# A mixture of experts whose token lists are made inside the expert stage: one list three experts ahead, places in eight rows of 64

## The reference

```
x = x + attention_relative(layernorm(x))
x = x + mixture(layernorm(x))
x = x + attention_window(layernorm(x))
x = x + mixture(layernorm(x))
```

```
scores = softmax(flat_x @ gate_w.T).T              # 16 x 4096
topk_weight, topk_idx = top_k(scores, C)           # each expert takes its 512 best tokens
xg = flat_x[topk_idx]                              # 16 x 512 x 256
h  = gelu(xg @ Wg.T) * (xg @ Wu.T)                 # hidden width 1024
eo = (h @ Wd.T) * topk_weight[..., None]
out = zeros.at[topk_idx].add(eo) + (gelu(x @ Sg.T) * (x @ Su.T)) @ Sd.T
```

## Time and profile before

| | before |
|---|---|
| median of three runs | 4274.7 us (4270.0 to 4282.5) |
| profiled execution: own time | 4275.8 us |
| profiled execution: span | 4274.0 us |
| mean granted TensorE clock | 0.942 |
| TensorE busy | 3662.2 us (86%), 32904 matmul records |
| VectorE busy | 2491.0 us (58%) |
| ScalarE busy | 1835.0 us (43%) |
| GpSimd busy | 780.0 us (18%) |
| DMA | 424 MB, mean 99 GB/s |

### The profile page before, as it was taken

The page is one execution under the profiler, slowest core; times in us unless marked ns, Lnnn a source line. Parts: engine busy times, 40 slices in busy tenths (PEclk is TensorE's granted clock), DMA queues, the critical chain, the costliest instruction groups (busy, mean ns, idle before and its releaser), DMA issues. The chain is left out here.

```text
span 4274.0 us, 91482 instructions
## 1 busy us (share of the span) xinstructions
PE 3662.2 (86%) x32904; PEld 2899.8 (68%) x32904; DVE 2491.0 (58%) x5053; ACT 1835.0 (43%) x3752; POOL 780.0 (18%) x714
## 2 busy tenths in 40 slices
PE   4899999999967848999956999888999695699998
PEld 3566666666556747888844777777777585588887
DVE  4466666666645695555544555444554467655554
ACT  1466666666612204444423444444444230244443
POOL 0122222222200003333310000000010000133332
PEclk9999999999988968999978999999999697799999
DMA  4566655665543204444331000000000420244442
GB/s 176 143 169 166 173 165 166 171 174 168 153 151 125 76 0 158 125 122 120 95 89 77 16 13 11 12 14 13 12 11 13 160 76 23 104 119 118 121 125 44
DMA packets 383916, 423.99 MB, mean 99 GB/s; under 512 B 172896, under 2 KB 323296, under 8 KB 370016
## 3 DMA queue, kind: packets, MB, share of 16 engines
q1 hardware_dynamic: 223840, 319.05, 22.8%
q10 hardware_dynamic: 135168, 67.13, 5.7%
q0 software_dynamic: 24576, 33.57, 4.9%
HBM read 269.37 MB, written 150.27 MB: 98 GB/s over the span
## 5 line engine op out<-in xcount | busy, mean ns | idle before, releaser
L2146 ACT ACTIVATE a_prob<-a_ps_s,a_low 128x512 f32<-128x512 f32 x512 | 319.0, 689 | 43.6 <-DVE a_low L2361 43.3
L2007 PE MATMUL a_ps_p<-a_ident,a_prob 128*128 128x128 f32 x2048 | 310.5, 285 | 24.9 <-ACT a_probT L2122 12.2
L2361 DVE TENSOR_REDUCE a_low<-a_ps_s 128x2 f32<-128x1024 f32 x256 | 313.5, 1225 | 8.8
L2221 POOL TENSOR_TENSOR a_below<-a_probT,a_upper 128x512 f32<-128x512 f32 x128 | 164.3, 1284 | 739.9 <-ACT a_probT L2122 370.4
L2007 PEld LDWEIGHTS a_ps_p<-a_ident,a_prob 128*128 128x128 f32 x2048 | 217.5, 141 | 119.0 <-issue 82.9
L2122 ACT COPY a_probT<-a_ps_p 128x512 f32<-128x512 f32 x352 | 194.1, 589 | 161.6 <-PE a_ps_p L2007 144.9
L1476 ACT ACTIVATE b_prob<-b_score,b_low 128x256 f32<-128x256 f32 (+1 forms) x512 | 240.6, 473 | 34.7 <-PE b_ps_p L1418 23.6
L1428 PEld LDWEIGHTS b_ps_o<-b_v,b_probT 128*128 128x128 f32 x1792 | 227.2, 191 | 9.9 <-issue 0.9
L1428 PE MATMUL b_ps_o<-b_v,b_probT 128*128 128x64 f32 x1792 | 228.3, 267 | 0.7 <-DVE b_o L1562 0.7
L1549 DVE CUSTOM_DVE_ANT_0 b_score<-b_ps_s,b_bias 128x256 f32<-128x256 f32 (+1 forms) x512 | 185.2, 389 | 56.5 <-PE b_ps_s L1409 37.2
L2360 DVE TENSOR_TENSOR a_ps_s<-a_ps_s,a_win 128x320 f32<-128x320 f32 (+1 forms) x256 | 135.0, 527 | 139.2 <-PE a_ps_s L2040 133.4
(11 more groups left out here) (400 smaller groups left out, 10581.3 us busy)
## 6 DMA issues: line engine op xcount, KB each, us to landing
a_win<-band SPq DMA_DIRECT2D x128, 384.0 KB, 4.9
prob<-a_prob ACTq DMA_DIRECT2D x128, 384.0 KB, 3.6
xnT<-n_xnT SPq DMA_DIRECT2D x32, 512.0 KB, 3.2
shift<-a_gbias SPq DMA_DIRECT2D x64, 256.0 KB, 2.0
a_shifted<-shift SPq DMA_DIRECT2D x256, 64.0 KB, 2.6
a_bins<-prob ACTq DMA_DIRECT2D x128, 128.0 KB, 4.5
fe_gT<-in_WgT SPq DMA_DIRECT2D x16, 1024.0 KB, 4.9
fe_uT<-in_WuT SPq DMA_DIRECT2D x16, 1024.0 KB, 5.3
```

The source lines that it names most:

```text
L2007: last = nc.tensor.transpose(bank[:, c * P:(c + 1) * P], prob[:, t % 2, h, 32 + c * P:32 + (c + 1) * P], ident[:, :])
L2146: nc.scalar.activation(prob[:, t % 2, h, 32:32 + T], ps_s[pair][:, r, :], ACT.Exp, bias=low[:, h:h + 1]).then_inc(exped, 1)
L2221: nc.gpsimd.tensor_tensor(below[:, t % 2, :, :], probT[:, t % 2, :, t * P:(t + 1) * P], upper[:, :].unsqueeze(1).to_broadcast([P, HG, P]), ...
L2361: nc.vector.reduce_max(low[:, 2 * pair:2 * pair + 2], both[:, :, :], AX.X, negate=True).then_inc(maxed, 1)
```

## The change

`route_stage` is deleted. Its set-up part (counts, scans, places, turning back) stands at the head of the expert stage's VectorE and TensorE programs; its per-expert part is a set of small steps spread over the eight steps of an expert, for the list of expert e + 3 (AHEAD = 3). Lists 0, 1 and 2 are made before VectorE's first product, between the splits of expert 0's weights and tokens. A place is now cut into place mod 64 (LOW) and place / 64 (8 hits), so that a list takes 32 matmuls of 24 weight columns by 64 moving columns; two more small float32 matmuls against the identity then place the 24 x 64 result on 128 partitions. `onehot` is written in quarters of 8 blocks. One PSUM bank `ps_x` serves both halves of the turned tokens (k = 0 at j = 4, k = 1 at j = 5), and the freed bank holds `ps_r` with the counts, `ps_f` and `ps_s`. GpSimd's gather of an expert waits for its list. The scratch tiles of the set-up lie in tiles that the experts use later. Both tables of the counts are loaded ahead of the identity, and the weights behind the five tables.

```diff
-def route_stage(nc, tag, const, scores, st, thr, slot_token, slot_weight):
...
+    LOW = 64
+    HITS = CAP // LOW
+    COLS = 3 * HITS
+    AHEAD = 3
+    QUARTERS = 4
+    M = NT * B // QUARTERS
...
-        X_STEP = 5
+        X_STEP = 4
+        FOUND_STEP = 3
+        TAKE_STEP = 7
...
+            for tile, dram in loads[0:2]:
+                sp.dma_start(tile, const[dram]).then_inc(const_in, 16)
...
+            for tile, dram in loads[2:]:
+                sp.dma_start(tile, const[dram]).then_inc(const_in, 16)
             for m in range(3):
                 load(0, m)
...
             def gather(e, q):
+                hold(pool, list_ready, e + 1, held)
                 take_index(0, e, q)
...
+            def transpose_rows(i, q, e, k):
+                if k == 0:
+                    pe.wait_ge(gathered[q], DONE * i + DONE)
+                pe.wait_ge(x_split, KC * e + KC + k)
+                for t in range(CT):
+                    last = nc.tensor.transpose(ps_x[:, t * P:(t + 1) * P], xg[:, q, t, k * P:(k + 1) * P], ident[:, :])
+                last.then_inc(x_T, 1)
+            def find(r, quarter):
+                if quarter == 0:
+                    pe.wait_ge(value_ready, 3 * r + 3)
+                    if not (isinstance(r, int) and r == 0):
+                        pe.wait_ge(list_ready, r)
+                pe.wait_ge(hot_ready, QUARTERS * r + quarter + 1)
+                for m in range(M * quarter, M * quarter + M):
+                    last = nc.tensor.matmul(ps_f, value[:, m, :, :, :].rearrange("p a v c -> p (a v c)"), onehot[:, m, :],
+                                            start=(m == 0), stop=(m == NT * B - 1))
+                if quarter == QUARTERS - 1:
+                    last.then_inc(found_ready, 1)
+            def place_slots(r):
+                pe.wait_ge(found_taken, r + 1)
+                for a in range(2):
+                    last = nc.tensor.matmul(ps_s[LOW * a:LOW * a + LOW, :, :].rearrange("p v c -> p (v c)"), found[:, :],
+                                            ident[0:COLS, 3 * CT * a:3 * CT * a + 3 * CT], start=True, stop=True)
+                last.then_inc(listed, 1)
...
+                    if first and j == 1:
+                        for quarter in range(QUARTERS):
+                            find(AHEAD - 1, quarter)
+                        place_slots(AHEAD - 1)
+                    if j == 0 and is_within(i, q, 1, E - AHEAD):
+                        place_slots(e + AHEAD - 1)
+                    if FOUND_STEP <= j < FOUND_STEP + QUARTERS and is_within(i, q, 0, E - 1 - AHEAD):
+                        find(e + AHEAD, j - FOUND_STEP)
+                    if not last and X_STEP <= j < X_STEP + KC:
+                        transpose_rows(i + q, 1 - q, e + 1, j - X_STEP)
...
+            for r in range(AHEAD - 1):
+                for quarter in range(QUARTERS):
+                    find(r, quarter)
+                place_slots(r)
+            for k in range(KC):
+                transpose_rows(0, 0, 0, k)
+            pe.wait_ge(parts_taken, 2)
+            every_expert(nc.tensor, expert)
...
+            slot_of = lambda k, r: partsT[:, k, :, :].rearrange("p t (b e) -> p (t b) e", e=E)[:, :, ds(r, 1)]
+            def hits(r, ch):
+                tile_of = slot_of(0, r)
+                ch.link(nc.vector.tensor_tensor(mine[:, :, :, :].rearrange("p m a c -> p m (a c)"), tile_of.to_broadcast([P, NT * B, HITS]),
+                                                halves[:, :].unsqueeze(1).to_broadcast([P, NT * B, HITS]), ALU.is_equal))
+                for k in range(3):
+                    part = token[:, :].unsqueeze(2) if k == 0 else weight[:, k - 1, :, ds(r, 1)]
+                    nc.vector.tensor_tensor(value[:, :, :, k, :], mine[:, :, :, :], part.unsqueeze(3).to_broadcast([P, NT * B, 2, CT]),
+                                            ALU.mult).then_inc(value_ready, 1)
+            def hot(r, quarter):
+                m = slice(M * quarter, M * quarter + M)
+                nc.vector.tensor_tensor(onehot[:, m, :], slot_of(1, r)[:, m, :].to_broadcast([P, M, LOW]),
+                                        iota[:, 0:LOW].unsqueeze(1).to_broadcast([P, M, LOW]), ALU.is_equal).then_inc(hot_ready, 1)
+            def take(r):
+                dve.wait_ge(found_ready, r + 1)
+                nc.vector.tensor_copy(found[:, :], ps_f).then_inc(found_taken, 1)
+            def lists(r, ch):
+                dve.wait_ge(listed, r + 1)
+                of = lambda x: x[:, ds(r, 1), :].rearrange("p a c -> p (a c)")
+                ch.link(nc.vector.tensor_copy(of(slot_token), ps_s[:, 0, :]))
+                ch.link(nc.vector.tensor_copy(of(slot_weight), ps_s[:, 1, :]))
+                nc.vector.tensor_tensor(of(slot_weight), of(slot_weight), ps_s[:, 2, :], ALU.add).then_inc(list_ready, 1)
...
                     rest_dve(nc, dve, step, j % RING, raw, h, hh_ready, hs_ready)
+                    if j == 0 and is_within(i, q, 0, E - 1 - AHEAD):
+                        hits(e + AHEAD, ch)
+                    if j == 1 and is_within(i, q, 1, E - AHEAD):
+                        lists(e + AHEAD - 1, ch)
+                    if 1 <= j <= QUARTERS and is_within(i, q, 0, E - 1 - AHEAD):
+                        hot(e + AHEAD, j - 1)
+                    if j == TAKE_STEP and is_within(i, q, 0, E - 1 - AHEAD):
+                        take(e + AHEAD)
+                    if more and X_STEP <= j < X_STEP + KC:
+                        split_x(e + 1, 1 - q, j - X_STEP)
                     if j == LAG - 1 and not first:
                         finish(e - 1, 1 - q, i + q - 1, early)
...
+            def whole_list(r):
+                hits(r, ch)
+                for quarter in range(QUARTERS):
+                    hot(r, quarter)
+            whole_list(0)
+            for m in range(0, UP // 2):
                 split_w(0, 0, m)
-            split_x(0, 0)
-            expert(0, 0, first=True)
-            expert(0, 1, early=True)
-            expert(1, 0, early=True)
+            take(0)
+            lists(0, ch)
+            whole_list(1)
+            for m in range(UP // 2, UP):
+                split_w(0, 0, m)
+            take(1)
+            lists(1, ch)
+            for k in range(KC):
+                split_x(0, 0, k)
+            for m in range(UP, EACH):
+                split_w(0, 0, m)
+            whole_list(2)
+            take(2)
+            lists(2, ch)
+            SETUP = ch.n
```

More of the change, by code:

```diff
@@ L917, in expert_stage @@
         eo = s.sb("eo", [P, 2, CT, C])
-        ps_x = [s.ps(f"ps_x{k}", [P, T]) for k in range(KC)]
+        partsT = s.sb("partsT", [P, 2, NT, P])
+        weight = s.sb("weight", [P, 2, NT * B, E])
+        mine = s.sb("mine", [P, NT * B, 2, CT])
+        value = s.sb("value", [P, NT * B, 2, 3, CT], F32R)
+        onehot = s.sb("onehot", [P, NT * B, LOW], F32R)
+        found = s.sb("found", [COLS, LOW])
+        halves = s.sb("halves", [P, HITS])
+        count = s.sb("count", [P, 1])
+        need = s.sb("need", [P, 1])
+        offset = s.sb("offset", [P, 1])
+        ones, work = gelu[:, 0, :], gelu[:, 1, :]
+        sel, pos = raw[:, 0, :], raw[:, 1, :]
+        parts = eo[:, 0, :, :].rearrange("p t c -> p (t c)").rearrange("p (k x) -> p k x", k=2)
+        equal = eo[:, 1, :, :].rearrange("p t c -> p (t c)")[:, 0:T]
+        posi = xg[:, 0, :, :].rearrange("p t c -> p (t c)").rearrange("p (k x) -> p k x", k=2).bitcast(I32)
+        tables = xg[:, 1, :, :].rearrange("p t c -> p (t c)")
+        same, before = tables[:, 0:P], tables[:, P:2 * P]
+        ps_x = s.ps("ps_x", [P, T])
+        ps_r = s.ps("ps_r", [P, T])
         ps_g = [s.ps(f"ps_g{q}", [P, T]) for q in range(2)]
@@ L1029, in down, with expert @@
                 down_pe(nc, pe, step, j % RING, h, by_block, j, HB, ps_d, hs_ready, down_done)
-            def expert(i, q, first=False, more=True):
+            def expert(i, q):
                 e = 2 * i + q
+                first, last = isinstance(e, int) and e == 0, isinstance(e, int) and e == E - 1
                 pe.wait_ge(w_split, EACH * e + UP)
@@ L1068, in split_w, with split_x, expert @@
                 nc.scalar.copy(high, w).then_inc(w_high, 1)
-            def split_x(e, q):
-                for k in range(KC):
-                    act.wait_ge(x_T, KC * e + k + 1 + KC)
-                    nc.scalar.copy(xs[0][:, q, k, :], ps_x[k][:, :]).then_inc(x_high, 1)
-            def expert(i, q, more=True):
+            def split_x(e, q, k):
+                act.wait_ge(x_T, KC * e + k + 1 + KC)
+                nc.scalar.copy(xs[0][:, q, k, :], ps_x[:, :]).then_inc(x_high, 1)
+            def expert(i, q):
                 e = 2 * i + q
+                more = not (isinstance(e, int) and e == E - 1)
                 for j in range(HB):
@@ L1081, in expert @@
                     mine = pieces_at(j) if more else ()
-                    for m in mine[:1]:
+                    for m in mine:
```

(1 more changed line is left out.)

272 lines of the change are left out of this document (93 added, 179 removed).

## The result

Four runs of the changed kernel beside four of the kernel before, on one chip: 4196.3 us (4193.5 to 4205.5) against 4272.4 (4269.8 to 4282.5), a ratio of 0.983 (0.981 to 0.985). The forecast was 4191. Later the changed kernel was run again beside another set: 4200.4 against 4265.8, 0.985 (0.983 to 0.987). The profiled execution after took 4194.8 us, 81 less than the one before.

The account below looks back on a forecast made before the run. VectorE sets the start's length, TensorE bounds the experts. Per mixture the start saves 83.5 us and experts pay 41.8: net 41.7, 83.4 in two, from 4275.8 to 4192.4, 4191 us on the median's scale; range 4160 to 4240.

Parts of the forecast that it names:

- the two mixtures' gain: Both mixture stages: 83.5 us less start minus 41.8 us more in the experts, net 41.7 each, 83.4 in two.
- The start: First table load to H(0) of a mixture: 44.4 us instead of 132.0; 83.5 us saved after 4.1 lost at H(2).
- List 2: Made on VectorE before its first product: H(2) starts at 56.0, 4.1 us lost, 11 to 12 us after H(0).
- The period: `finish` to `finish` of two experts: 38.1 us instead of 34.9; forecast wrong if under 36.5 or above 39.5.
- D(0)'s wait: TensorE waits 1.9 us for `finish`, 0.7 plus 1.25 from `lists` and one `hot` ahead of it in step 1.
- `hits` hidden: VectorE around step 1's product: 1.6 us of `hits` fits 1.37 us idle because `place_slots` moves H(1) 0.45 later.
- find: TensorE, each expert: 32 matmuls of 64 moving columns at 45 ns, 1.45 us.
- place_slots and turning: TensorE, each listing expert: 0.45 us for placing the list, 0.1 us for turning the tokens in two halves.
- The clock: TensorE's granted clock inside the experts stays 1.00.
- The rival: TensorE's clock falls in every expert from the longer gap before D(0): 52 to 130 us more; chance 0.05, split with "same".
- GpSimd, SyncE and ScalarE get no further work: In the experts, these three engines get nothing added; GpSimd's gather of e + 2 starts as now.
- the sum: Unhidden expert costs: 3.25 us for experts 1 to 12, 39.0, plus experts 0, 13 and 14: 41.8 us per mixture.

Follow-up runs that it names:

- finish_first: Changed kernel with `finish` of the expert before put ahead of the lists and first `hot` in step 1, behind weight piece and hidden rest: 4172.3 us, 0.976.
- finish_early: Changed kernel with `finish` of the expert before put right behind the product of step 1: 4147.5 us, 0.972.
- the shifts: Extra TensorE instructions ahead of stage b: 56 or 152 in the changed kernel, 4176.7 and 4192.7 us; 200 in the kernel before, 4289.4 us.
- two experiments: Changed kernel with each small matmul of `find` issued twice, 4247.8 us; changed kernel with four more comparisons beside `hits` at j = 0, 4231.1 us.

## Why the prediction was right, and where it was not

The total, 4191 against 4196.3, is right within 0.13%, and that closeness is luck: the mixtures gained 8 us more than forecast, stage b lost 21 that no step held, and stage a gave 11 by chance. The mechanism, a start of 44 us bought with 3 us in each of twelve experts, is as forecast; the two mixtures' gain, 91.5 us against 83.4, is the fair measure of it.

- **The start**: 44.4 forecast, 44.0 measured; the gather reached TensorE at 38.8 us, 39.5 forecast, and the two halves of the tokens followed as laid out. List 2 cost 2.5 us instead of 4.1: H(2) starts 10.0 us after H(0), 11 to 12 forecast. 85.5 us per mixture instead of 83.5.
- **The period**: 38.1 forecast, 37.8 measured; D(0)'s wait 1.9 forecast, 1.86 measured; `hits` hidden with 0.34 us to spare, as forecast; VectorE's share 63%, 64 forecast. `finish_first` and `finish_early` show that the wait is worth what it lasts, and 0.3 us more.
- **find**: 45 ns was wrong, 31 ns is right (1.0 us for 32, not 1.45). What went wrong is the choice between bounds: I took a value between 28 and 104, though the old line of the same type ran at what streaming asks and the 104 came from another type. The Trainium skill ("TensorE: Matmul & The Clock Gate", section "Wait — 56ns, not 53.3ns?") has about 62 ns for a TensorE whose sequencer decodes the matmuls; with 31 ns at 64 columns that case is not seen here. Its 25 ns is not contradicted.
- **place_slots and turning**: 0.55 forecast. In `finish_early`, without any wait, a listing expert takes 35.65 us and one without a list 33.97 (before the change 34.89 with a wait of 0.68 and those 0.3, so the same); less 1.0 for `find` that leaves 0.7. So cheap matmuls and dear placing nearly cancel, and an expert pays 2.9 us instead of 3.25.
- **The clock**: called 1.00 throughout; it falls once in each mixture, 1.6 us each. The rival had a fall that does occur, but neither its frequency nor its price: it asked for one in every expert, 52 to 130 us, where two falls cost 3 us.
- **What was missing**: that a change shifts the code behind it. "GpSimd, SyncE and ScalarE get no further work" and "the sum" counted only stages that the change edits. No term stood for it, and the 21 us in b are as large as half of what a mixture gains. A sign of the same kind was in the kernel before, TensorE's five waits for ScalarE's `b_oT`, but nothing could be read from it ahead of the shifts.

## What to carry to other kernels

When an untouched stage changes its length between two versions, look for waits on nothing once in a loop's round, and count the instruction loads in it, and shift the loop by some instructions before explaining it otherwise: here that was worth 34 us of b's length, nearly half of what the whole change brought. Put what frees a buffer for the bound engine (`finish`) ahead of preparatory work on the same engine: 2.2 us an expert for moving two lines. And read an added-work experiment by its steady period, not by its total: in two experiments the total fit a wrong price, since short falls of the clock filled the difference.

## What the hardware showed that I had not expected

- f32r matmuls of 24 weight columns and 64 moving ones, each with its own weights, follow one another every 31 ns at the granted clock of 1.00, where those of 128 columns took 60.
- A loop of 1738 instructions stays in TensorE's memory or has blocks fetched again in every round, by where it begins: one or no block in 590 us with its start at 73 of a block, 40 or 41 at 17 and at 169. Most of the stalls that come with it are 2.0 to 2.7 us, and the clock falls behind them: b's turning unit takes 30.8 us without a stall and 37.3 with two, 2.0 us more than the stalls.
- A short fall of the clock in otherwise dense experts (a mean of 0.96 over the expert) costs 1.6 us each time; a wait of 0.7 us in every expert brought none, one of 2.4 us five in a mixture.
